# Moving the routing into the operand stage, single maximum items between the pieces of expert tiles, and half of the spline weights formed by TensorE

## The chip, the cores and the metric

The kernel runs on one core of one Trainium2 chip. The metric is the time of one execution on the device in microseconds. Inputs and outputs are in the device's memory; the core has the engines TensorE (PE), VectorE (DVE), ScalarE (ACT) and GpSimd (POOL), and SyncE (SP), whose queue issues most transfers.

## The reference

Four layers act on a sequence batch of 4 by 1024 tokens with 256 channels. Each layer normalises its input and adds an attention and a feed-forward result to it. What bears on the change:

```python
# layer 0: x + attention(xn) + experts(xn)
sh_mid = gelu(xt @ Wsh_up[e]); shared_out = sum_e sh_mid @ Wsh_down[e]     # 2 shared experts
probs = softmax(xt @ W_router)                                            # 16 routed experts
top_v, top_i = top_k(probs, 2)
routed_out = sum over the two chosen experts: (gelu(xt @ Wrt_up[e]) * top_v) @ Wrt_down[e]
# layer 1, feed-forward: gate_w, up_w (1024 x 256) and down_w (256 x 1024) are read off control points
w = 0.5 * (2*p1 + (p2 - p0)*f + (2*p0 - 5*p1 + 4*p2 - p3)*f**2 + (3*p1 - p0 - 3*p2 + p3)*f**3)
```

Layers 2 and 3 (a recurrent mix with ternary weights; an attention with low-rank experts) are not touched.

## The kernel before

Each layer first brings its weights in, and then loops over the four sequences of the batch. A layer's loop is a row of stages; a stage is a block in which every engine has its own list of instructions, tied by semaphores, with a barrier of all engines at its end. 1024 tokens are 8 tiles of 128.

**Layer 0's loop** has three stages.
1. `attention_operands` normalises the tokens, turns them (`m.xn_t`), projects each tile to queries, keys and values (L417, TensorE), adds the bias (L438, L439) and rotates queries and keys (L464 to L469, VectorE), splits them in halves of lower precision (L507, L509 ScalarE; L537, L538 GpSimd), turns these (L403) and stores them (L487). TensorE issues in tile `t` the projection of `t` and the turn of `t - 2`.
2. `experts` does three things at once. `Routing` makes the router's logits (L1189), softmax, the two best experts of each token and from their counts the slot of each token in a list that is sorted by expert and padded to 32 tiles of 128 slots (L1222 to L1272 on VectorE in five parts, L1199 to L1206 on TensorE). GpSimd scatters the tokens into their slots in memory (L1450), the SP queue fetches slots and the weights of each slot tile's expert (L1457, L1463). The shared experts run on all tokens (`up`, L1313, `gelu`, L1389, `down`, L1323, and the additions, L1424). Then the 32 slot tiles go through their expert in 16 pairs: `tile_turn` (L1335), `tile_up_products` (L1346), Gelu (L1407), `tile_down` (L1356), copy (L1415), and the store. Third, `MaximumPass` finds the row maxima of the attention's scores: TensorE forms the scores of a pair of maps over up to 512 keys (L606 the mask, L610 the product) and VectorE reduces them (L642). There are 96 such items and 4 "turn" items (L595, L637), which bring the maxima of a group of maps in place. Items use two pairs of PSUM banks in turn, so an item's matmuls wait for VectorE to be done with the item before the last.
3. `attention` takes the scores again, applies the exponential and adds up the values; `combine` adds the routed experts' results.

The order is written out by hand. `share_out` spreads the 100 items over named places in the lists of TensorE, VectorE and SP:

```python
ahead = [(("route", i), LEAD, (4, 6)) for i in range(Routing.PARTS)] + [(("scatter",), WAITING, (4, 6))]
rest = len(mp.items) - LEAD * Routing.PARTS - WAITING
mp.share_out(ahead + [(("tiles", i), rest / (pairs + 2), (4, 6)) for i in range(pairs + 2)], 2)
```

With `LEAD` 2 and `WAITING` 20, two items stand in each of five places among the routing parts and the shared experts, 20 in the place in which the scatter runs, and the other 70 in the loop over tile pairs: about four in a row between `tile_up_products(i - 1)` and `tile_down(i - 2)`.

**Layer 1's `spline_weights`** runs once, ahead of the loop. The weights are a sum of six basis tiles of 128x256, each times one scalar per row. 24 units (16 for gate and up, two on one basis tile, and 8 for down, one each) are made one after the other: VectorE scales the first (L1539) and adds five more (L1541), TensorE turns the result (L1553), ScalarE copies it twice (L1564, L1565), GpSimd subtracts (L1572). The SP queue brings the basis tiles into a ring of two.

## Time and profile before

| | |
|---|---|
| median of 3 runs | 4731.2 us (4724.24 to 4739.67) |
| the profiled execution | 4727.96 us |
| its span, first to last instruction | 4726.2 us |
| busy in the span: TensorE, VectorE, ScalarE, GpSimd | 3558.2, 2655.8, 1832.9, 669.3 us |
| mean granted clock of TensorE | 0.874 of full speed |

A row of the trace gives an instruction's line in the kernel, its engine and operation, out<-in by the program's names, and times in us from the span's start. PE is a matmul, PEld the load of its weights. `x4` counts instructions; a matmul in 32-bit floats is two records. `[1.79 <-PE ps L610]` is the idle time of that engine ahead of the row and what ended it.

### The profile page before, as it was taken

The numbers are of one execution on the slowest core, as the hardware profiler recorded it, in microseconds if no ns is written. First come the engines' busy times: TensorE is split into PE (matmuls) and PEld (weight loads), VectorE is DVE, ScalarE is ACT, GpSimd is POOL, SyncE is SP. The second block draws the span as 40 slices with busy tenths as digits, with TensorE's granted clock in tenths as the row PEclk, the third lists the DMA queues.
The fourth block names the chain that finished last, engine by engine and source line by source line (L and its number), as shares of the span: only waits on it lengthen the run. The fifth ranks groups of instructions, "written<-read, shape, count | busy, mean of one in ns | idle before, by whom it ended". The sixth has DMA issues, their size and how long they took to land. (4 is left out here: it accounts for less than half of the span.)

```text
span 4726.2 us, 61082 instructions
## 1 busy us (share of the span) xinstructions
PE 3558.2 (75%) x22176; PEld 2132.8 (45%) x22176; DVE 2655.8 (56%) x5412; ACT 1832.9 (39%) x2729; POOL 669.3 (14%) x814
## 2 busy tenths in 40 slices
PE   5676766767358787786865777866897797797797
PEld 3424344243123636344352645645572572572573
DVE  5656566566664543645436446454763764664664
ACT  3272542725254362634512323322306306306306
POOL 2011110121110000001000202202230230230230
PEclk8897988879679998898986988978899899899899
DMA  3403204033300000000020000001000000000000
GB/s 108 136 25 112 81 27 149 29 99 95 119 26 1 10 10 10 10 1 19 1 69 9 9 9 18 0 18 59 15 1 10 10 1 10 10 1 10 10 1 10
DMA packets 133505, 159.37 MB, mean 34 GB/s; under 512 B 16160, under 2 KB 109856, under 8 KB 133152
## 3 DMA queue, kind: packets, MB, share of 16 engines
q1 hardware_dynamic: 121712, 132.18, 8.7%
q0 software_dynamic: 6144, 16.79, 1.1%
q10 hardware_dynamic: 5328, 6.30, 0.4%
q8 instruction: 180, 2.95, 0.3%
q14 instruction: 141, 1.16, 0.1%
HBM read 108.57 MB, written 47.19 MB: 33 GB/s over the span
## 5 line engine op out<-in xcount | busy, mean ns | idle before, releaser
L642 DVE TENSOR_REDUCE arena<-ps 128x2 f32<-128x1024 f32 (+3 forms) x768 | 694.7, 951 | 175.3 <-PE ps L610 172.2
L831 ACT ACTIVATE arena<-ps 128x1024 f32<-128x1024 f32 (+3 forms) x768 | 570.9, 813 | 74.3 <-PE ps L744 68.6
L912 DVE TENSOR_TENSOR arena<-arena,tri 128x256 f32<-128x256 f32 x512 | 211.8, 424 | 300.6 <-ACT arena L831 293.9
L761 PE MATMUL ps<-arena 128*17 128x512 f32 (+3 forms) x3072 | 334.0, 507 | 6.7 <-DVE arena L912 4.0
L831 ACT ACTIVATE attention<-ps 128x1024 f32<-128x1024 f32 (+3 forms) x384 | 287.9, 809 | 131.0 <-PE ps L744 130.9
L744 PE MATMUL ps<-arena 64*128 64x512 f16 (+3 forms) x1536 | 252.0, 343 | 105.7 <-ACT arena L831 65.3
L2027 ACT ACTIVATE arena<-ps 128x256 f32<-128x256 f32 x192 | 63.9, 381 | 616.2 <-PE ps L1969 576.5
L610 PE MATMUL ps<-arena 64*128 64x512 f16 (+3 forms) x1536 | 239.0, 348 | 68.6 <-DVE arena L642 68.0
L761 PE MATMUL ps<-attention 128*33 128x512 f32 (+3 forms) x1536 | 289.1, 499 | 0.0
L744 PEld LDWEIGHTS ps<-arena 64*128 64x128 f16 x1536 | 69.9, 93 | 447.8 <-ACT arena L831 375.1
L417 PE MATMUL ps<-arena 128*128 128x512 f32 (+1 forms) x768 | 267.0, 497 | 0.0
L2099 POOL TENSOR_TENSOR arena<-arena 128x256 f32<-128x256 f32 x192 | 139.3, 725 | 511.2 <-DVE arena L2052 511.2
L1957 PE MATMUL ps<-arena 128*128 128x256 f32 x768 | 207.5, 393 | 1.8 <-DVE arena L2052 1.8
L1008 PE MATMUL ps<-ffn_parts,weight_parts 128*128 128x512 f32 x768 | 188.3, 407 | 14.9 <-DVE ffn_parts L1090 14.9
L1126 DVE TENSOR_TENSOR ffn<-ffn,ps 128x512 f32<-128x512 f32 x128 | 87.4, 683 | 195.3 <-ACT ffn L1071 117.7
L417 PEld LDWEIGHTS ps<-arena 128*128 128x128 f32 x768 | 143.5, 194 | 101.3 <-issue 94.9
L912 DVE TENSOR_TENSOR attention<-attention,tri 128x256 f32<-128x256 f32 x256 | 103.1, 424 | 144.0 <-ACT attention L831 143.8
L1008 PEld LDWEIGHTS ps<-ffn_parts,weight_parts 128*128 128x128 f32 x768 | 149.0, 195 | 54.0 <-DVE ffn_parts L1090 17.8
L606 PE MATMUL ps<-mask_col,mask_row 64*128 64x64 bf16 x2048 | 118.1, 198 | 67.5 <-DVE arena L642 66.8
L606 PEld LDWEIGHTS ps<-mask_col,mask_row 64*128 64x128 bf16 x2048 | 69.7, 96 | 191.2 <-DVE arena L642 129.0
L1957 PEld LDWEIGHTS ps<-arena 128*128 128x128 f32 x768 | 137.6, 189 | 37.3 <-issue 15.6
L1071 ACT ACTIVATE ffn<-ps 128x512 f32<-128x512 f32 x128 | 76.0, 594 | 198.0 <-PE ps L1008 198.0
(301 smaller groups left out, 6701.5 us busy)
## 6 DMA issues: line engine op xcount, KB each, us to landing
arena<-w_experts SPq DMA_DIRECT2D x128, 256.0 KB, 3.2
arena<-slots_x SPq DMA_DIRECT2D x32, 512.0 KB, 4.4
slots_y<-arena SPq DMA_DIRECT2D x32, 512.0 KB, 4.1
x_next<-sums SPq DMA_DIRECT2D x15, 1024.0 KB, 5.4
sums<-arena SPq DMA_DIRECT2D x24, 512.0 KB, 2.8
making<-basis SPq DMA_DIRECT2D x16, 768.0 KB, 4.5
x_next<-x SPq DMA_DIRECT2D x5, 1024.0 KB, 5.8
slots_x<-arena SPq DMA_DIRECT2D x1, 4096.0 KB, 15.3
```

The costliest lines, as they stand in the source:

```text
L417: last = pe.matmul(m.ps[:, 2 * (t % 2) + j, 0:w], m.xn_t[:, k, t * P:(t + 1) * P], wqkv[:, k, c0:c0 + w], start=(k == 0), stop=(k == KD - 1))
L606: pe.matmul(out[:, odd, w - P + H * i:w - P + H * i + H], m.mask_row[half, i, :], m.mask_col[half, i, half], start=(i == 0), stop=False, s ...
L610: last = pe.matmul(out[:, odd, 0:w], a.q[half, pair, qt * P:(qt + 1) * P], a.k[half, pair, c * CH:c * CH + w], start=not diag, stop=True, ...
L642: dve.reduce_max(a.mp[:, 2 * j:2 * j + 2, qt, c], out[:, :, 0:w], AX.X).then_inc(self.pair_out, 1)
L744: last = pe.matmul(m.ps[:, 4 + 2 * (v % 2) + odd, q0:CH], a.k[half, pair, kt * P:(kt + 1) * P], a.q[half, pair, c * CH + q0:(c + 1) * CH], ...
L761: last = pe.matmul(m.ps[width * hh:width * hh + w, unit % 2, q0:CH], a.v[:, kt, vh, :], a.p[:, (pairs * n + hh // 2) % ring, hh % 2, q0:CH ...
L831: act.activation(a.p[:, v % ring, :, q0:CH], m.ps[:, b:b + 2, q0:CH], ACT.Exp, scale=HD ** -0.5).then_inc(exped, 1)
L912: dve.tensor_tensor(diag, diag, keep, ALU.min).then_inc(masked, 1)
L1008: last = pe.matmul(m.ps[:, 2 * (n % 3) + j, :], w[wp][:, k, i * P:(i + 1) * P], f.x[:, xp, k, c * CH:(c + 1) * CH], start=(k, (wp, xp)) == ...
L1126: dve.tensor_tensor(f.inter[:, n % 3, :], f.gate[:, n % 2, :], m.ps[:, 2 * (n % 3) + 1, :], ALU.mult).then_inc(gated, 1)
L1957: pe.matmul(part(n, j), wt[:, k, i * P:(i + 1) * P], m.xn_t[:, k, columns(q)], start=(j == 0 and k == 0), stop=False, skip_group_check=True)
L2099: pool.tensor_tensor(f.h[:, r, n % 3, :], f.h[:, r, n % 3, :], f.wb[:, r, columns(q)], ALU.mult).then_inc(weighted, 1)
```

## The change

- The constants `LEAD` and `WAITING` go; `AHEAD` is 7.
- `Routing` runs in `attention_operands` when it is given: the logits on TensorE ahead of the projection of tile 2, in free columns of a bank of that projection; parts 0 to 3 on VectorE at the ends of tiles 2 to 5; the exponential on ScalarE behind tile 2; the rank matmuls behind the projection of tile 7; part 4 behind VectorE's last tile.
- `experts` begins with the scatters (GpSimd) and the weight and slot fetches (SP). The shared experts have four places of seven items, and each iteration over tile pairs has four places, between halves of `tile_up` and of `tile_down`, with one item in most of them.
- Buffers move: the routing's behind the operand stage's scratch, `f.mid` behind the attention's memory, the slots onto that scratch.
- In `spline_weights` every second unit is formed by TensorE: VectorE writes six diagonal matrices (the identity times a scalar per row) and TensorE multiplies the six basis tiles by them into one sum, which comes out turned. Four PSUM banks in place of two, a ring of four basis tiles in place of two.

```diff
@@ attention_operands
             norm.tensor(pe)
             pe.wait_ge(*weights)
             for t in range(NT):
...
                 if t == 2:
                     pe.wait_ge(norm.stored, NT // 2)
+                    if routing is not None:
+                        routing.tensor_logits(pe)
+                if t == 4 and routing is not None:
+                    pe.wait_ge(routing.shifted, 1)
...
+            if routing is not None:
+                pe.wait_ge(taken, 2 * (NT - 1))
+                routing.tensor_ranks(pe, 0)
             for t in range(NT - lag, NT):
                 turn(t)
...
+                if routing is not None and 2 <= t < 6:
+                    routing.vector(dve, t - 2)
+            if routing is not None:
+                routing.vector(dve, 4, 0)
...
+                if t == 2 and routing is not None:
+                    routing.scalar(act)
@@ experts
-        ahead = [(("route", i), LEAD, (4, 6)) for i in range(Routing.PARTS)] + [(("scatter",), WAITING, (4, 6))]
-        rest = len(mp.items) - LEAD * Routing.PARTS - WAITING
-        mp.share_out(ahead + [(("tiles", i), rest / (pairs + 2), (4, 6)) for i in range(pairs + 2)], 2)
+        ahead = 4 * AHEAD
+        rest = len(mp.items) - ahead
+        mp.share_out([(("shared", i), AHEAD, (4, 6)) for i in range(4)] +
+                     [(("tiles", i, p), rest / (4 * pairs + 4), (4, 6)) for i in range(pairs + 1) for p in range(4)], 1)
...
-            routing.tensor_logits(pe)
             pe.wait_ge(*weights)
             up(0, 0)
-            mp.tensor_share(pe, ("route", 0))
             up(0, 1)
-            mp.tensor_share(pe, ("route", 1))
+            mp.tensor_share(pe, ("shared", 0))
             up(1, 0)
             up(1, 1)
+            mp.tensor_share(pe, ("shared", 1))
             down(0)
-            mp.tensor_share(pe, ("route", 2))
+            mp.tensor_share(pe, ("shared", 2))
             down(1)
-            mp.tensor_share(pe, ("route", 3))
-            routing.tensor_ranks(pe, 0)
-            mp.tensor_share(pe, ("route", 4))
-            mp.tensor_share(pe, ("scatter",))
+            mp.tensor_share(pe, ("shared", 3))
             pe.wait_ge(added, NT)
             for i in range(pairs + 2):
                 if i < pairs:
                     tile_turn(i)
                 if 1 <= i <= pairs:
-                    tile_up_products(i - 1)
-                mp.tensor_share(pe, ("tiles", i))
+                    tile_up(i - 1, 0)
+                mp.tensor_share(pe, ("tiles", i, 0))
+                if 1 <= i <= pairs:
+                    tile_up(i - 1, 1)
+                mp.tensor_share(pe, ("tiles", i, 1))
                 if i >= 2:
-                    tile_down(i - 2)
+                    tile_down(i - 2, 0)
+                mp.tensor_share(pe, ("tiles", i, 2))
+                if i >= 2:
+                    tile_down(i - 2, 1)
+                mp.tensor_share(pe, ("tiles", i, 3))
...
             pool.wait_ge(m.slots_zeroed, 16)
-            pool.wait_ge(routing.placed, 1)
...
-            for part in range(Routing.PARTS):
-                mp.sync_share(sp, ("route", part))
-            sp.wait_ge(routing.tiles_known, 1)
             for i in range(4):
                 fetch_weights(i)
-            mp.sync_share(sp, ("scatter",))
             sp.wait_ge(m.scattered, 16 * 2 * NT)
             for g in range(4):
                 fetch_slots(g)
+            for i in range(4):
+                mp.sync_share(sp, ("shared", i))
@@ spline_weights, vector
             for i, (n, win, out) in enumerate(units):
-                dve.wait_ge(basis_in[n % 2], 16 * (n // 2 + 1))
-                if i >= 2:
-                    dve.wait_ge(turned, i - 1)
+                if i >= 4:
+                    dve.wait_ge(turned, i - 3)
+                if i % 2 == 1:
+                    for s in range(NSEG):
+                        ins = dve.tensor_scalar(f.diag[:, i // 2 % 2, s, :], m.ident[:, :], win[:, s:s + 1], None,
+                                                ALU.mult)
+                    ins.then_inc(spread, 1)
+                    continue
+                dve.wait_ge(basis_in[n % ring], 16 * (n // ring + 1))
...
@@ spline_weights, tensor
+                else:
+                    pe.wait_ge(basis_in[n % ring], 16 * (n // ring + 1))
+                    pe.wait_ge(spread, i // 2 + 1)
+                    for k in range(KD):
+                        for s in range(NSEG):
+                            last = pe.matmul(m.ps[:, i % 4, k * P:(k + 1) * P],
+                                             f.basis[:, n % ring, s, k * P:(k + 1) * P], f.diag[:, i // 2 % 2, s, :],
+                                             start=(s == 0), stop=(s == NSEG - 1))
                 last.then_inc(turned, 1)
```

## Rows read from the trace of the kernel before

**Rows 1.** Stretches: operand stage, experts stage of the first and second batch.
```profile
core 0: us, PE busy (x) PEld busy (x) DVE busy (x) ACT busy (x) POOL busy (x), PEclk, DMA share, GB/s
23.00:72.30 49.30, 33.72 (x208) 22.52 (x208) 36.00 (x74) 30.77 (x35) 14.78 (x20) 0.94 0.09 31
72.30:230.00 157.70, 106.72 (x832) 70.38 (x832) 101.89 (x167) 30.58 (x56) 15.71 (x16) 0.80 0.41 128
372.30:527.00 154.70, 104.00 (x832) 67.90 (x832) 101.89 (x167) 30.56 (x57) 15.42 (x16) 0.82 0.42 130
```

**Rows 2.** Order of time, front of the experts stage, first batch.
```profile
80.80 3.42 PE L1313 MATMUL ps<-arena 128*128 128x512 f32 x4
...
87.05 3.70 PE L1313 MATMUL ps<-arena 128*128 128x512 f32 x8
...
104.19 1.31 POOL L1450 DMA_INDIRECT slots_x<-arena  x1 [35.76 <-DVE arena L1267]
...
123.51 0.96 POOL L1450 DMA_INDIRECT slots_x<-arena  x1 [0.30 <-issue]
...
132.06 1.09 PE L1335 MATMUL ps<-ident,arena 128*128 128x128 f32 x4 [6.74 <-DMA arena<-slots_x]
```

**Rows 3.** Stretch of the logits, L1189 alone: TensorE, weight loads, granted clock.
```profile
73.95:80.95 7.00, 6.97 (x32) 6.90 (x32) 0.50 0.50 153
```

**Rows 4.** Groups from 132 to 222: count, busy, mean ns, idle before.
```profile
L642 DVE TENSOR_REDUCE arena<-ps 128x2 f32<-128x512 f32 (+3 forms) x67 | 60.4, 956 | 32.2 <-PE ps L610 31.9
```

**Rows 5.** Order of time in one iteration over tile pairs.
```profile
161.93 0.60 PE L1335 MATMUL ps<-ident,arena 128*128 128x128 f32 x4
...
162.37 1.06 PE L1346 MATMUL ps<-arena 128*128 128x128 f32 x8
...
163.36 0.39 PE L610 MATMUL ps<-arena 64*128 64x512 f16 x2
...
163.79 1.56 DVE L642 TENSOR_REDUCE arena<-ps 128x2 f32<-128x1024 f32 x2 [1.79 <-PE ps L610]
...
165.68 1.13 PE L1356 MATMUL ps<-arena 128*128 128x256 f32 x4
...
166.64 0.60 PE L1335 MATMUL ps<-ident,arena 128*128 128x128 f32 x4
```

**Rows 6.** Order of time in the first operand stage.
```profile
32.76 7.91 PE L417 MATMUL ps<-arena 128*128 128x512 f32 x24
...
45.56 1.07 PE L403 MATMUL ps<-ident_h,arena 128*128 128x128 f16 x16 [0.17 <-POOL arena L538]
...
45.82 0.69 DVE L469 TENSOR_TENSOR arena<-arena 128x512 f32<-128x512 f32 x1
...
65.18 0.69 DVE L469 TENSOR_TENSOR arena<-arena 128x512 f32<-128x512 f32 x1
```

**Rows 7.** Stretches of routing part 4 on VectorE, and all five parts' sum.
```profile
100.72:104.94 4.22, 0.39 (x6) 0.14 (x6) 3.88 (x15) 0.00 (x0) 0.75 (x1) 0.92 0.00 0
sum 8.59, PE 4.76 PEld 2.70 DVE 8.02 ACT 2.11 POOL 0.75; mean PE 0.95 PEld 0.54 DVE 1.60 ACT 0.42 POOL 0.15
```

**Rows 8.** The instructions of L467: duration ns, least, median and most.
```profile
L467 DVE TENSOR_TENSOR arena<-arena,sin x64: 416/884/889, 37.6 to 4414.8; 128x256 f32<-128x256 f32 x64
```

**Rows 9.** Stretch from VectorE's last record to the attention's first.
```profile
223.90:230.10 6.20, 0.77 (x2) 0.08 (x2) 0.01 (x1) 0.64 (x2) 0.00 (x0) 0.50 0.26 87
```

**Rows 10.** Groups of VectorE in the spline stage.
```profile
L1541 DVE SCALAR_TENSOR_TENSOR making<-making 128x256 f32<-128x256 f32 x120 | 65.9, 549 | 4.3
...
L1539 DVE TENSOR_SCALAR making<-making 128x256 f32<-128x256 f32 x24 | 8.4, 349 | 24.8 <-DMA making<-basis 24.8
```

**Rows 11.** Order of time: first and last record of the spline stage's work.
```profile
1229.56 0.35 DVE L1539 TENSOR_SCALAR making<-making 128x256 f32<-128x256 f32 x1 [18.42 <-DMA making<-basis]
...
1314.58 0.72 POOL L1572 TENSOR_TENSOR weight_parts<-making,weight_parts 128x256 fp32r<-128x256 f32 x1 [3.88 <-ACT making L1565]
```

**Rows 12.** Two stretches of 4 us, among items and in the loop: granted clock.
```profile
112.00:116.00 4.00, 1.69 (x18) 0.68 (x16) 3.62 (x5) 0.00 (x0) 2.96 (x4) 0.50 0.97 347
148.00:152.00 4.00, 2.90 (x28) 1.87 (x28) 3.18 (x4) 0.81 (x3) 0.00 (x0) 1.00 0.59 156
```

More of the change, by code:

```diff
@@ L1337, in tile_turn @@
                 last.then_inc(turned, 1)
-            def tile_up_products(i):
-                pe.wait_ge(weights_in[i % 4], 32 * (i // 4 + 1))
-                pe.wait_ge(turn_kept, i + 1)
-                if i >= 1:
-                    pe.wait_ge(tile_gelued, i)
-                for half in range(2):
-                    for k in range(KD):
-                        last = pe.matmul(m.ps[:, 1, half * P:(half + 1) * P], f.w_tile[:, i % 4, half, k * F0:(k + 1) * F0],
-                                         f.slots_t[:, i % 2, k, half * P:(half + 1) * P], start=(k == 0),
-                                         stop=(k == KD - 1))
-                last.then_inc(tile_upped, 1)
@@ new lines, in tile_down @@
+            def tile_down(i, half):
+                if half == 0:
+                    pe.wait_ge(tile_gelued, i + 1)
+                    if i >= 2:
+                        pe.wait_ge(kept, i - 1)
+                last = pe.matmul(m.ps[:, 2 + i % 2, half * D:(half + 1) * D], f.tile_mid[:, i % 2, half * P:(half + 1) * P],
+                                 f.w_tile[:, i % 4, half, KD * F0:EXPERT], start=True, stop=True)
+                if half == 1:
+                    last.then_inc(tile_downed, 1)
@@ L1426, in _ @@
             mp.vector_start(dve)
-            routing.vector(dve, 0)
-            mp.vector_share(dve, ("route", 0))
-            routing.vector(dve, 1)
-            mp.vector_share(dve, ("route", 1))
-            routing.vector(dve, 2)
+            mp.vector_share(dve, ("shared", 0))
+            mp.vector_share(dve, ("shared", 1))
             add(0)
-            mp.vector_share(dve, ("route", 2))
-            routing.vector(dve, 3)
+            mp.vector_share(dve, ("shared", 2))
             add(1)
-            mp.vector_share(dve, ("route", 3))
-            routing.vector(dve, 4, 0)
-            mp.vector_share(dve, ("route", 4))
-            mp.vector_share(dve, ("scatter",))
+            mp.vector_share(dve, ("shared", 3))
             for i in range(pairs + 2):
-                mp.vector_share(dve, ("tiles", i))
+                for part in range(4):
+                    mp.vector_share(dve, ("tiles", i, part))
         @block.gpsimd
@@ L1484, in _ @@
                     fetch_weights(i + 2)
-                mp.sync_share(sp, ("tiles", i))
+                for part in range(4):
+                    mp.sync_share(sp, ("tiles", i, part))
                 if i >= 3 and i % 2 == 1:
@@ L1523, in _ @@
             for n, (kind, t) in enumerate(tiles):
-                if n >= 2:
-                    last_use = max(i for i, u in enumerate(units) if u[0] == n - 2)
-                    sp.wait_ge(formed, last_use + 1)
+                if n >= ring:
+                    sp.wait_ge(turned, max(i for i, u in enumerate(units) if u[0] == n - ring) + 1)
                 src = basis_gu[t] if kind == "gu" else basis_d[t // 4][t % 4]
-                sp.dma_start(f.basis[:, n % 2, :, :], src).then_inc(basis_in[n % 2], 16)
+                sp.dma_start(f.basis[:, n % ring, :, :], src).then_inc(basis_in[n % ring], 16)
         @block.vector
@@ L2204, in program @@
             f.tile_weights = ar.take(SLOT_TILES, dtype=U32)
-            at = ar.at
-            f.mid = ar.take(E_SH * NC, CH)
-            ar = Arena(arena, at)
+            f.mid = Arena(arena, a.end).take(E_SH * NC, CH)
+            ar = Arena(arena, a.free)
             f.slots = ar.take(4, 4, D)
@@ L2236, in program @@
                 f.win = ar.take(3, F1 // P, NSEG)
-                f.basis = ar.take(2, NSEG, D)
+                f.basis = ar.take(4, NSEG, D)
+                f.diag = ar.take(2, NSEG, P)
                 f.w = ar.take(2, D)
```

97 lines of the change are left out of this document (51 added, 46 removed).

## The prediction

> **What bounds the kernel now.** I read the stretches by stage first, then the order of time inside the experts stage, then the groups of VectorE, then the granted clock in short stretches. The change touches the first layer, whose batch loop runs four times, and one stage of the second layer that runs once. One batch of the first layer takes an operand stage of 49.3 us, an experts stage of 157.7 us (154.7 us in the second batch) and an attention stage [rows 1]. The experts stage is over half of the batch, and in it no engine is full: VectorE works 101.9 us, TensorE 106.7 us, GpSimd 15.7 us [rows 1].
>
> The order of time says why. The stage opens with 7.0 us of router logits on TensorE, in which VectorE has nothing [rows 3]. The slots of the tokens are known only at 104.2, where GpSimd starts sixteen scatters that end at 124.5, and TensorE stands 6.7 us until the first slots are back at 132.1 [rows 2]. Up to there the pairs of expert tiles can't begin. From 132 on the stage is a loop over 16 pairs. In it VectorE has 67 maximum reductions of 0.956 us in the mean and is idle 32.2 us ahead of them, always for L610 [rows 4] (6.7 us of that is the slot wait again, so 25.5 us are the loop's own). One iteration shows where they come from [rows 5]: TensorE turns (0.44 us, start to start), makes the two up products (0.99), issues four items in a row, of which the third and fourth wait for VectorE to free a PSUM pair, and makes the down products (0.96). While the 2.4 us of tile work run, VectorE has two items left and then stands 1.8 us. The iteration takes 4.71 us. So the loop is bound by neither engine, but by their taking turns.
>
> **The operand stage.** VectorE sets its pace: from its L469 at 45.82 to the one five tiles on at 65.18 are 3.87 us a tile, without a gap; but TensorE too has only 0.17 us of slack per tile [rows 6]. After the last rotation at 65.18 come copies, transposes and stores to 72.3 [rows 1, 6]: 6.4 us in which VectorE is free.
> Added here are the logits, ahead of the third projection, and routing parts 0 to 3 on VectorE after tiles 2 to 5. These parts took 8.59 less 4.22, that is 4.37 us [rows 7]. The logits are 32 records, 6.97 us at half clock [rows 3], so an estimate of 3.5 us at the full one. TensorE ends its third projection at 40.67, and VectorE is ready for it when its L469 one tile before 45.82 ends, at 42.6 [rows 6]: 1.9 us are covered, 1.6 stay as a new wait of VectorE at tile 2. The exponential waits on ScalarE behind `high(2)`; with its table load it keeps ScalarE some 1.6 us from `store(1)`, which is wanted a tile later, and that tile has just been stretched by as much. It costs nothing, and at most 1.6 us. The rank matmuls (under 1 us) stand between two `turn`s in a gap of the tail. Part 4, 4.22 us, runs in the 6.4 us after the last rotation: free. Sum +6.0 us per batch; from +4.4 (logits hidden) to +10 (the clock falls in the logits and one or two projections run at half speed).
> L467 takes 0.42 us at the least and 0.88 us in the median, where GpSimd's subtraction runs beside it [rows 8]; part 4 now meets the last two such subtractions, and a VectorE instruction of 0.3 to 0.7 us could hold each back. I leave this inside the bound. The Trainium skill, SBUF — State Buffer, section "SBUF: two separate sides", says that the two engines share a port pair which one holds for a whole instruction; by it the tail would be 0.5 to 1.4 us longer, some 4 us over four batches, and the trace agrees on the doubled duration.
>
> **The experts stage.** I rebuild it from VectorE. Its 101.9 us lose the routing's 8.0 busy us [rows 1, 7]: 93.9. Added to that are its idle times:
> - At the start the first two up products. One took 3.42 us at half clock, two took 3.70 at the full one [rows 2]: 1.9 to 3.4 for the second, with the first item 6.4 us in all.
> - The shared part is now blocks: seven items, 3.7 us of TensorE work, seven items, and so on, three such blocks. While one runs VectorE finishes one or two items, and stands about 2.1 us: 6.3. Between blocks TensorE is lightly used; with some of the work at half clock another 3 (0 to 6).
> - The scatters start at once. They take 20.3 us as now (104.2 to 124.5), the landing and the fetch of the slots 7.6 as now (to 132.1): ready 28 us into the stage. The shared part has 28 items by 0.956, the additions and the idle above, 42 us. So the slot wait, 6.7 us now, goes, with 14 us to spare. The weight fetches and `x_next` are now in the queue in front; at the 312 GB/s that 128 GB/s at a share of 0.41 stands for [rows 1], those 3.1 MB take 10 us, also inside the margin.
> - In the loop an item stands between any two pieces. TensorE's work in an iteration is 0.44 + 0.99 + 0.96 and four items of about 0.25, 3.4 us; VectorE's is four items, 3.8 us. The longest piece ahead of an item is turn and half an up product, 0.93 us, about one reduction. What stays is a short hand-over around the narrow items, an estimate of 0.1 us for each of the 68: 7 (0 to the 25.5 of now). TensorE comes in at half clock and, at some 6 us per iteration there, is behind until it rises: 3 (0 to 6).
> - The end. From VectorE's last record to the next stage's first is 6.2 us [rows 9], with the last turn 7.
> Sum 93.9 + 6.4 + 6.3 + 3 + 7 + 3 + 7 = 126.6 us. Before it is 157.7 and 154.7 less the 1.7 us of barrier ahead of the first record, mean 154.5. Saved 27.9, less 6.0, that is 21.9 per batch and 88 in all.
>
> **The spline weights.** Now 24 units, each one L1539 and five L1541 on VectorE (0.349 and five by 0.549), from 1229.56 to 1315.3, 85.7 us [rows 10, 11]. L1539 waits 24.8 us for basis tiles, 18.4 of them for the first, so 6.4 us inside the stretch; the rest is a pace of 3.2 us a unit. After, every second unit is six 128x128 scalings on VectorE. A 128x256 one takes 0.349; a row of half the width isn't there, so 0 to 0.349 bounds each, and I take 0.24, 1.45 us a unit. A pair of units is 4.7 us on VectorE, twelve are 56. TensorE has per pair two transposes and twelve matmuls: 24 records of 0.22 us at half clock (6.97 by 32), 5.3 us and 0.7, and about half of that at the full one. It would be the slower at half clock, but is then full. The ring of four tiles takes the waits away but for some 2 us. With start and end (the last unit's matmuls, 3 to 5 us, are bare) 65 us against 85.7: 20 saved, from 6 (half clock throughout, 12 by 6 and the ends) to 28.
>
> **Sum.** The profiled execution took 4728.0 us, its span 4726.2; the median is 4731.2, 0.07% above. 4728 - 88 - 20 = 4620.
>
> **The rivals.**
> - *Better hand-over.* No idle in the loop and no slow clock: 126.6 - 7 - 3 - 3 = 113.6, operand stage +4.4: 36.5 by 4 and 28 are 174, so 4554. For it: one item per piece fits almost exactly. Against: narrow items can't hide 0.93 us of TensorE.
> - *Half clock in half of the loop.* An iteration is then about 6.4 us by TensorE in place of 4.1. Eight of them cost 18, less the 3 counted: 142 us, so 6.5 by 4 and 20 are 46: 4682. For it: the clock is 0.50 while TensorE is busy 1.7 of 4 us between items [rows 12]. Against: with 2.9 of 4 it is 1.00 there.
> - *The tiles' weights or slots come too late.* Shorter iterations fetch the same bytes. If landing takes the iteration back to 5 us, only the front of the stage gains: 140 us, 4674. Against: share 0.41 now [rows 1], and only the first slots are waited for.
> - *Slower: TensorE at half clock all through the loop.* The place is the loop, the price 2.3 us per iteration. 17 iterations and the shared blocks (8 us) give 126.6 + 36 + 8 = 171, so 16 + 6 lost per batch, 6 won in the splines: 4810. It decides from 12 of 17 iterations at half clock, since 12 by 2.3 by 4 are the 108 us won. In the logits TensorE is busy without a break and still at 0.50 [rows 3], so being busy is not enough. The Trainium skill, TensorE: Matmul & The Clock Gate, "HAM oscillation — how this bites in real kernels", has idle gaps bring the slow state back each time; gaps in the loop get shorter and more frequent, so it speaks rather for the fast state, and the row from 148 on agrees.
> - *No change*, by several of the bounds at once.
>
> **How the numbers follow.** Forecast 0.52 (its own range 4590 to 4650), better hand-over 0.16, half clock in part 0.13, late transfers 0.07, slower 0.05, no change 0.03, and between the cases 0.04. The range of 4560 to 4680 reaches to the good case and to the half-clock one. A measurement tells 0.3%, 14 us, from no change. Faster 0.92, same 0.03, slower 0.05.
>
> **What would show it.** Operand stage 55 us in place of 49, with a wait of VectorE for L417 at tile 2 and part 4 ahead of the stage's last copies. Scatters in the first 21 us of the experts stage, no wait of TensorE for slots. In the loop iterations near 4.2 us with VectorE over 90% busy and the clock at 1.00. In the spline stage a TensorE that is busy most of the time. The prediction is wrong if VectorE still stands over 1 us per iteration, if the clock is 0.50 beyond the first iterations, or if the operand stage grows over 10 us.

## The result, and the profile after

The changed kernel takes 4620.9 us in the median of 4 runs (4615.4 to 4623.7), against 4733.0 us (4 runs, 4724.2 to 4739.7) of the kernel before, measured beside it. The ratio is 0.9763, with a 95% interval of 0.9744 to 0.9782: 2.4% faster. The profiled execution took 4622.5 us, its span 4620.8 us.

In the kernel after, lines are L448 and L449 for the bias, L474 to L479 for the rotation, L1205 for the logits, L658 for the maximum, L626 for the scores of an item, L1326 and L1336 for the shared products, L1348, L1359 and L1369 for turn, up and down of the expert tiles, L1440 for the additions.

Stretches of the kernel after: operand stage and experts stage of the first batch [rows 1], then the second split at the first turn and at the end of the last long group of maximum items.

```profile
core 0: us, PE busy (x) PEld busy (x) DVE busy (x) ACT busy (x) POOL busy (x), PEclk, DMA share, GB/s
23.00:76.30 53.30, 38.10 (x256) 27.90 (x256) 42.18 (x120) 32.37 (x37) 14.20 (x20) 0.91 0.08 29
76.30:205.80 129.50, 103.65 (x784) 60.14 (x784) 94.84 (x121) 28.94 (x53) 15.74 (x16) 0.91 0.50 155
78.00:123.30 45.30, 32.11 (x185) 16.69 (x185) 26.59 (x39) 3.67 (x5) 15.74 (x16) 0.80 0.48 163
123.30:196.60 73.30, 69.43 (x589) 42.31 (x588) 65.56 (x78) 24.07 (x46) 0.00 (x0) 0.99 0.56 166
196.60:205.80 9.20, 2.11 (x14) 1.14 (x13) 2.69 (x6) 1.20 (x2) 0.00 (x0) 0.88 0.17 59
```

The same split of the kernel before:

```profile
80.80:132.10 51.30, 31.04 (x212) 15.03 (x213) 37.65 (x87) 5.26 (x7) 15.71 (x16) 0.70 0.30 100
132.10:220.40 88.30, 66.77 (x578) 47.29 (x578) 61.43 (x74) 23.44 (x47) 0.00 (x0) 0.91 0.49 152
220.40:230.10 9.70, 2.09 (x12) 1.24 (x13) 2.70 (x6) 0.64 (x2) 0.00 (x0) 0.67 0.17 56
```

VectorE's idle time is a row's length less its busy time. In the loop, the second row of the split, VectorE was idle 26.9 us and is idle 7.7. (The later batches differ less: the second batch's loop took 85.4 us before, and 73.4 after.) In the first row it was idle 13.7 and is idle 18.7, but it has 11 us less to do there, and the 7 us of logits ahead of the row are gone. The operand stage is 4.0 us longer. One iteration of the loop, in order of time, in place of [rows 5]:

```profile
158.51 0.66 PE L1348 MATMUL ps<-ident,arena 128*128 128x128 f32 x4
159.00 0.61 PE L1359 MATMUL ps<-arena 128*128 128x128 f32 x4
...
159.61 0.22 PE L626 MATMUL ps<-arena 64*128 64x128 f16 x2
159.76 0.71 PE L1359 MATMUL ps<-arena 128*128 128x128 f32 x4
...
160.68 0.70 PE L1369 MATMUL ps<-arena 128*128 128x256 f32 x2
160.79 0.69 DVE L658 TENSOR_REDUCE arena<-ps 128x2 f32<-128x512 f32 x1 [0.42 <-PE ps L626]
...
162.64 0.55 PE L1348 MATMUL ps<-ident,arena 128*128 128x128 f32 x3
```

It takes 4.13 us in place of 4.71, and VectorE's gaps are 0.4 us or less. The front of the experts stage, in place of [rows 2]:

```profile
78.04 6.73 PE L1326 MATMUL ps<-arena 128*128 128x512 f32 x8 [3.94 <-PEq L64]
...
78.97 1.31 POOL L1459 DMA_INDIRECT slots_x<-arena  x1 [6.81 <-issue]
...
98.32 0.96 POOL L1459 DMA_INDIRECT slots_x<-arena  x1 [0.30 <-issue]
99.09 6.07 PEld L1336 LDWEIGHTS ps<-arena 128*128 128x128 f32 x16 [0.25 <-issue]
99.09 6.47 PE L1336 MATMUL ps<-arena 128*128 128x256 f32 x16
101.58 2.04 SPq L1466 DMA_DIRECT2D arena<-slots_x  x4
102.91 0.76 DVE L1440 TENSOR_TENSOR arena<-ps,arena 128x256 f32<-128x256 f32 x2 [3.02 <-PE ps L1336]
```

The scatters run beside the shared experts, the slots are fetched at 101.6, and the loop starts at 123.3 without a wait for them.

Over four batches the saving reads off one mark in SP's queue, the issue of `x_next<-sums` that ends the fourth batch. Before it stands at 1215.15 and after at 1126.76: 88.4 us. From there to the issue of `making<-lq`, which follows the spline stage, are 101.1 us before (to 1316.29) and 83.6 after (to 1210.37): 17.5 us. The spans of the two traces differ by 105.4 us, their medians by 112.

### The profile page after: what moved, and what is told of

It is laid out like the page before. It is cut to its first block and busy times, and to the rows that moved or that the text cites. A ratio compares the mean times of both kernels' runs of the same rounds, so it can differ in the third digit from the quotient of the medians.

```text
span 4620.8 us, 61585 instructions
## 1 busy us (share of the span) xinstructions
PE 3602.9 (78%) x22440; PEld 2160.3 (47%) x22440; DVE 2635.4 (57%) x5412; ACT 1832.0 (40%) x2725; POOL 666.1 (14%) x814
## 5 line engine op out<-in xcount | busy, mean ns | idle before, releaser
L658 DVE TENSOR_REDUCE arena<-ps 128x2 f32<-128x1024 f32 (+3 forms) x768 | 696.7, 951 | 107.3 <-PE ps L626 102.8
L626 PE MATMUL ps<-arena 64*128 64x512 f16 (+3 forms) x1536 | 233.1, 329 | 31.0 <-DVE arena L658 30.1
L1983 PEld LDWEIGHTS ps<-arena 128*128 128x128 f32 x768 | 137.7, 189 | 37.2 <-issue 15.7
L2078 DVE TENSOR_TENSOR arena<-arena,ps 128x256 f32<-128x256 f32 x192 | 79.7, 415 | 123.0 <-ACT arena L2053 123.0
```

The lines of the kernel that those rows point to most:

```text
L626: last = pe.matmul(out[:, odd, 0:w], a.q[half, pair, qt * P:(qt + 1) * P], a.k[half, pair, c * CH:c * CH + w], start=not diag, stop=True, ...
L658: dve.reduce_max(a.mp[:, 2 * j:2 * j + 2, qt, c], out[:, :, 0:w], AX.X).then_inc(self.pair_out, 1)
L1983: pe.matmul(part(n, j), wt[:, k, i * P:(i + 1) * P], m.xn_t[:, k, columns(q)], start=(j == 0 and k == 0), stop=False, skip_group_check=True)
```

## The experiments

All times in this table are in us. "Mark" is the issue of `x_next<-sums`. "Loop" is the first batch's stretch from the first turn to the last long maximum group, with VectorE's idle time in it. Each kernel was timed beside the kernel before, whose median moved by up to 3 us from one time to the next; so differences of 3 us between medians in this table say nothing.

| kernel | median (runs) | mark | loop, idle |
|---|---|---|---|
| before | 4729.9 to 4733.2 (four times, 4 to 9 runs each) | 1215.2 | 88.3, 26.9 |
| after | 4620.9 (4) | 1126.8 | 73.3, 7.7 |
| spline_alone | 4708.3 (5) | 1213.6 | 84.2, 22.7 |
| items_alone | 4685.8 (4) | 1166.8 | 72.5, 9.5 |
| four_in_a_row | 4677.2 (4) | 1187.1 | 87.5, 22.7 |
| two_and_two | 4623.8 (4) | 1126.5 | 72.9, 7.5 |
| long_and_short | 4638.1 (4) | 1140.6 | 77.4, 12.4 |
| three_and_one | 4650.5 (4) | 1154.8 | 79.5, 14.0 |
| parts_late | 4639.9 (4) | 1145.8 | 73.4, 7.8 |
| fine_shared | 4590.7 (5) | 1094.7 | 74.9, 8.7 |
| diag_scalar | 4602.0 (5) | 1131.8 | 73.3, 7.9 |
| both | 4567.6 (5) | 1092.7 | 74.9, 8.5 |

### The three parts of the change, one at a time

**spline_alone** is the kernel before with the new `spline_weights` and its buffers. Of the edit only the buffers are shown:

```diff
...
-                f.basis = ar.take(2, NSEG, D)
+                f.basis = ar.take(4, NSEG, D)
+                f.diag = ar.take(2, NSEG, P)
```

> The kernel before with the new spline weights alone (diagonals and TensorE for half of the tiles, four basis buffers); routing and items stay as before. From the traces of before and after, the time from the first spline unit on VectorE to the last copy fell from 85.7 to 68 us. Theory (the three parts of the change add up): 17 us faster than before, 4716 us, within 4 either way. Rival (the spline's gain was partly that of another clock or of another arrival of the basis after the new fourth batch): under 10 us, 4723 or more.

Measured 4708.3, 4 us below the range of 4712 to 4720. The ratio is 0.9946 (0.9933 to 0.9960), that is 19 to 32 us by the runs. The profile gives the part itself: from mark to `making<-lq` 83.6 us, the same as in the changed kernel, so 17.5 us; the two traces' spans differ by 18.5. The theory holds for the stage; the medians moved by more than the traces account for, and that excess stays open.

**items_alone** is the kernel before with `tile_up` and `tile_down` in halves and an item place behind each. Routing and splines stay. Of the edit only the sharing out is shown:

```diff
...
-        mp.share_out(ahead + [(("tiles", i), rest / (pairs + 2), (4, 6)) for i in range(pairs + 2)], 2)
+        mp.share_out(ahead + [(("tiles", i, p), rest / (4 * pairs + 4), (4, 6)) for i in range(pairs + 1) for p in range(4)], 1)
```

> The kernel before with the interleaved item places in the loop of expert tiles alone; routing stays in the experts stage, spline weights stay as before. Theory: VectorE's idle time in the loop goes from 27.7 to about 8 us, 20 us per batch, 80 in all: 4650 to 4660 us; moving the routing is then worth the rest of what the experts and operand stages gained (88), about 2 us per batch net. Rival (the routing's move paid more than that, as VectorE's front part of the experts stage lost its routing operations of some 20 us while the operand stage took only 4): 4665 us or more.

Measured 0.9897 (0.9882 to 0.9913), 47 us; the mark moved by 48.4, 12.1 per batch. So the rival's time held. The theory's 20 us per batch were too many: the 27.7 us that I had read as the loop's idle time before reached to 223.9 and so had some 3 us behind the last items in it, the loop of this kernel still idles 9.5 us, and VectorE works 1.6 us more in it. The loop is 15.8 us shorter in the first batch, and 12.6 in the second (72.8 in place of 85.4). The slots are still waited for here, 6.7 us ahead of the loop. Its row:

```profile
132.50:205.00 72.50, 69.94 (x577) 42.47 (x578) 63.05 (x75) 24.04 (x46) 0.00 (x0) 0.96 0.61 185
```

**four_in_a_row** is the changed kernel with the four places put together:

```diff
                 if 1 <= i <= pairs:
                     tile_up(i - 1, 0)
-                mp.tensor_share(pe, ("tiles", i, 0))
-                if 1 <= i <= pairs:
                     tile_up(i - 1, 1)
-                mp.tensor_share(pe, ("tiles", i, 1))
+                for p in range(4):
+                    mp.tensor_share(pe, ("tiles", i, p))
                 if i >= 2:
                     tile_down(i - 2, 0)
-                mp.tensor_share(pe, ("tiles", i, 2))
-                if i >= 2:
                     tile_down(i - 2, 1)
-                mp.tensor_share(pe, ("tiles", i, 3))
```

> The changed kernel with the four item places of a pair of expert tiles put together again, between the up and the down products, as in the kernel before; routing in the operand stage and the new spline stay, and the number of items per pair stays. Theory (VectorE's idle time in the loop is hand-over: TensorE's products of 1.9 and 0.6 us lie in one piece while VectorE has nothing ready): VectorE's idle time in the loop goes from 7.8 back to about 26 us, so 17 to 20 us per batch, 70 to 80 in all: 4690 to 4700 us. Rival (the gain of the loop came from routing being gone and from TensorE's clock staying at 1.0, not from the order): under 5 us per batch, 4640 or less.

```profile
128.30:215.80 87.50, 65.86 (x586) 46.74 (x584) 64.85 (x79) 22.95 (x46) 0.00 (x0) 0.93 0.45 139
```

Measured 4677.2, 56 us above the changed kernel: 14 per batch, between the theory's 17 to 20 and the rival's 5, and nearer the theory. The idle time came back, 22.7 us in the first batch and 20.9 in the second. 4.4 us of the 56 are a lower clock in the operand stage of the first batch (last section). The order of the items is thus worth some 52 us by the medians on top of the routing's move, and 56 by the marks (60.3 less 4.4); without the move it is worth 48. By the marks, routing in the operand stage alone gave 28.1, or 32.5 without those 4.4; items alone gave 48.4; together they gave 88.4. The 7.5 us more than the sum are 1.9 per batch, and nothing here says from what. The granted clock of this loop is 0.93, against 0.99 in the changed kernel; what part of the 14 us is the clock's was not separated.

### How many items, and where

**two_and_two** moves the places to behind the up products and behind the down products, two items each. Against four_in_a_row:

```diff
                     tile_up(i - 1, 1)
-                for p in range(4):
-                    mp.tensor_share(pe, ("tiles", i, p))
+                mp.tensor_share(pe, ("tiles", i, 0))
+                mp.tensor_share(pe, ("tiles", i, 1))
                 if i >= 2:
                     tile_down(i - 2, 0)
                     tile_down(i - 2, 1)
+                mp.tensor_share(pe, ("tiles", i, 2))
+                mp.tensor_share(pe, ("tiles", i, 3))
```

> The changed kernel with the items of a pair of tiles in two places of two: two between the up and the down products, two after the down products. Two theories of what counts. A (only the longest unbroken stretch of TensorE's other products against the 1.9 us that VectorE has in hand with two bank pairs counts): turns and ups together are about 1.9 us of 4.2, downs about 0.5, so one long stretch per pair of tiles outlasts what VectorE has in hand by about 1 us; with 18 pairs about 10 to 14 us idle per loop rather than 7.8: 4630 to 4645 us. B (idle grows with the number of items in a row, four giving 26 and one 8): two give about 14 to 17, 4645 to 4660 us. C (order matters little): 4625 or less.

Measured 4623.8: C. Theory A fell by an error of its own: turn and up products are 1.43 us [rows 5], not 1.9. With the right figure it gives what was measured, since 1.43 and an item's 0.25 are within the 1.9 us of two reductions; but that figure was put in after the result. The next two kernels ask whether that sum predicts.

**long_and_short**: the two halves are unequal, 1.9 us of products in one stretch and 0.5 in the other, two items behind each.

```diff
                 if 1 <= i <= pairs:
                     tile_up(i - 1, 0)
                 mp.tensor_share(pe, ("tiles", i, 0))
+                mp.tensor_share(pe, ("tiles", i, 1))
                 if 1 <= i <= pairs:
                     tile_up(i - 1, 1)
-                mp.tensor_share(pe, ("tiles", i, 1))
+                mp.tensor_share(pe, ("tiles", i, 2))
+                mp.tensor_share(pe, ("tiles", i, 3))
                 if i >= 2:
                     tile_down(i - 2, 0)
-                mp.tensor_share(pe, ("tiles", i, 2))
-                if i >= 2:
                     tile_down(i - 2, 1)
-                mp.tensor_share(pe, ("tiles", i, 3))
```

> The changed kernel with the items again two and two, but the places moved: downs, turn and the first up product (1.9 us) in one stretch, two items, the second up product (0.5 us), two items. Theory (the stretch with the first item behind it, against two items in hand of 1.9 us): 0.25 us short per pair of tiles, some 4 us per batch, 4637 us (4630 to 4645). By the same sum four in a row are 2.4 + 0.25 - 1.9 = 0.75 us short, 13 us over 17 pairs of tiles, and its loop measured 13.5 us longer. Rival (two items in a row are as good as one wherever they stand): 4624 or less.

Measured 4638.1, loop 77.4: 4.1 us longer than the changed kernel's, as the sum said.

**three_and_one**: three items behind the up products, one behind the down products. Against two_and_two:

```diff
                 mp.tensor_share(pe, ("tiles", i, 1))
+                mp.tensor_share(pe, ("tiles", i, 2))
                 if i >= 2:
                     tile_down(i - 2, 0)
                     tile_down(i - 2, 1)
-                mp.tensor_share(pe, ("tiles", i, 2))
                 mp.tensor_share(pe, ("tiles", i, 3))
```

> The changed kernel with three items after the up products and one after the down products. The runs so far: with one item between any two pieces, and with two and two, VectorE is idle 7.5 to 7.7 us in the loop; with four in a row 20.9 to 22.7. Theory (what counts is that TensorE's stretch, with the first item behind it, is no longer than what VectorE still has in hand, two items of 0.95 us in the mean): turn and ups take 1.43 us start to start and downs 0.96. The longest run with little between is downs, one item, turn and ups, then an item: 0.96 + 0.25 + 1.43 + 0.25 = 2.9 us, against the two items in hand and the one made between, 2.85. So hardly any new idle time, 0 to 2 us per batch: 4621 to 4630 us. Rival (each gap of VectorE comes with how many items stand in a row, and three are nearer to four than to two): 8 to 10 us per batch, 4655 to 4665.

Measured 4650.5, loop 79.5: 6.2 us longer. The theory fell, and the rival is nearer but not right either (it asked for 8 to 10 us, and for 4655 or more). The order of time shows the step that it left out:

```profile
159.20 4.38 DVE L658 TENSOR_REDUCE arena<-ps 128x2 f32<-128x1024 f32 x4 [1.11 <-PE ps L626]
160.48 0.39 PE L626 MATMUL ps<-arena 64*128 64x512 f16 x2 [1.10 <-DVE arena L658]
160.80 1.13 PE L1369 MATMUL ps<-arena 128*128 128x256 f32 x4
```

The third item of a row finds no free PSUM pair, so TensorE stands 1.10 us in front of it, with the down products queued behind. Then it makes the item (0.39 us), in which VectorE already works on what it has. So VectorE has in hand two reductions less the making of the last, 1.5 us rather than 1.9, and less again where a narrow one is among them (they range from 0.40 to 1.23 us). This step is read from the order of time, and no kernel tests it: put into the sum for two and two (1.43 and 0.25 against 1.5), it asks for some 3 us more per batch, and that loop is not longer. TensorE's whole wait for VectorE in the loop tells the five orders apart:

| order | TensorE waits for VectorE | loop |
|---|---|---|
| one by one | 3.7 us | 73.3 |
| two and two | 8.2 | 72.9 |
| long and short | 11.6 | 77.4 |
| three and one | 16.5 | 79.5 |
| four in a row | 21.1 | 87.5 |

Its work in an iteration is 3.4 us against 3.8 of VectorE, some 7 us of slack in 17 iterations. By this account waits up to about that are free, and what lies beyond comes back: 11.6, 16.5 and 21.1 less 7 are 5, 9 and 14 us, where the loop grew by 4, 6 and 14. The account was made from these five traces, after the runs; it foretold none of them, and is 3 us off for three and one. The kernel before fits it as well, with 21.0 us of such waits and a loop of 88.3 us.

### The operand stage

**parts_late** leaves routing part 0 after tile 2 and puts parts 1 to 3 behind the last tile (and on TensorE, not shown, the rank products behind the last turn).

```diff
-                if routing is not None and 2 <= t < 6:
-                    routing.vector(dve, t - 2)
+                if routing is not None and t == 2:
+                    routing.vector(dve, 0)
             if routing is not None:
+                for part in range(1, 4):
+                    routing.vector(dve, part)
                 routing.vector(dve, 4, 0)
```

> The changed kernel with only the first routing part left after tile 2 of the operand stage; parts 1 to 3 come after the last tile on VectorE, and the rank products after all turns of TensorE. In the changed kernel the last rotation starts 3.7 us later than before, though 1.6 us of waiting and 4.4 us of routing were put ahead of it; the two products with the sine take 9.1 us in the stage rather than 12.5. Theory (they run beside GpSimd's subtraction of the tile before and are held by it; a routing part between them lets GpSimd finish first, so four parts cost VectorE less than their own time): with the parts gone from the tiles the two groups return to 11.5 to 12.5 us, and the last rotation starts near 67 (68.86 in the changed kernel, 65.18 before), not at 65.5, where it would be if 3.7 us were what the parts cost. Parts 1 to 4, about 8 us, then stand behind it and the stage ends 0.5 to 2 us later: 4623 to 4629 us. Rival (the routing parts simply took less time there than in the experts stage): the two groups stay near 9.1 us.

Rows of one tile in the changed kernel, after a routing part, and then its last tile, which no part precedes:

```profile
59.85 0.42 DVE L475 TENSOR_TENSOR arena<-arena,sin 128x256 f32<-128x256 f32 x1
60.19 0.42 DVE L477 TENSOR_TENSOR arena<-arena,sin 128x256 f32<-128x256 f32 x1
...
66.94 0.80 POOL L553 TENSOR_TENSOR arena<-arena 128x256 f16<-128x256 f32 x1 [2.60 <-ACT arena L523]
67.25 0.77 DVE L475 TENSOR_TENSOR arena<-arena,sin 128x256 f32<-128x256 f32 x1
67.70 0.84 POOL L554 TENSOR_TENSOR arena<-arena 128x256 f16<-128x256 f32 x1
67.94 0.88 DVE L477 TENSOR_TENSOR arena<-arena,sin 128x256 f32<-128x256 f32 x1
```

The two products with the sine over the first stage, changed kernel and then parts_late (least, median and most in ns):

```profile
L475 DVE TENSOR_TENSOR arena<-arena,sin x8: 425/599/777, 37.5 to 67.2; 128x256 f32<-128x256 f32 x8
L477 DVE TENSOR_TENSOR arena<-arena,sin x8: 411/418/885, 37.9 to 67.9; 128x256 f32<-128x256 f32 x8
```

```profile
L475 DVE TENSOR_TENSOR arena<-arena,sin x8: 424/774/778, 38.4 to 69.4; 128x256 f32<-128x256 f32 x8
L477 DVE TENSOR_TENSOR arena<-arena,sin x8: 410/883/886, 38.7 to 70.1; 128x256 f32<-128x256 f32 x8
```

The medians are back at 0.77 and 0.88 with the parts gone, and the two groups take 11.2 us in place of 9.1, just short of the 11.5 to 12.5 that the theory asked for. In the third batch (operand stage from 597 on), where the projections run alike in both kernels, the first to the last rotation are 30.6 us apart in the changed kernel and 28.5 in parts_late: parts 1 to 3, which take 3.9 us, cost 2.1. So the theory holds on where the time went. The last rotation can't be compared in the first batch, where the clock fell (last section). The Trainium skill, SBUF — State Buffer, section "SBUF: two separate sides", has VectorE and GpSimd exclude each other on a shared port pair for a whole instruction. These rows agree in direction, 0.42 us apart from the subtraction and 0.77 and 0.88 beside it; that the wait is a whole instruction they do not show.

The kernel is 19 us slower, where I had forecast 2 to 8. Split by stage, the move itself fits: where no clock falls, attention and operand stage together take 149.4 us (211.2 to 360.6) against 148.5 (205.8 to 354.3), 0.9 more. The rest goes with TensorE's granted clock, in places that the edit did not touch: 4.4 us each ahead of the third projection's end in the first and the fourth batch, and some 6 us together in the experts stages of the second and the third. First, second and third batch's loop of parts_late:

```profile
128.60:202.00 73.40, 69.53 (x590) 42.34 (x588) 65.65 (x79) 24.04 (x46) 0.00 (x0) 0.99 0.54 166
407.00:483.80 76.80, 73.54 (x590) 44.84 (x588) 65.88 (x79) 24.04 (x46) 0.00 (x0) 0.91 0.50 159
688.50:763.90 75.40, 71.92 (x590) 43.74 (x588) 65.69 (x79) 24.04 (x46) 0.00 (x0) 0.94 0.53 162
```

The changed kernel has 73.3 or 73.4 in all four batches. Whether the edit had a part in the clock's falls is open; without this split the 19 us would have been booked as the price of the move.

### The shared part, the diagonals, and both

**fine_shared**: twelve pieces and twelve places. Each pair of additions also comes as soon as its products are there, and TensorE's wait for them moves behind the up products of the loop's third iteration. Of the edit only the down products are shown:

```diff
...
-            down(0)
-            mp.tensor_share(pe, ("shared", 2))
-            down(1)
-            mp.tensor_share(pe, ("shared", 3))
-            pe.wait_ge(added, NT)
+            for n in range(NT):
+                down(n // TC, n % TC)
+                mp.tensor_share(pe, ("shared", 4 + n))
```

> The changed kernel with the shared experts' products cut into twelve pieces (four up products, eight token tiles of the down product) and the same 28 items spread over twelve places between them, in place of seven after each of four blocks; each addition comes as soon as its two down products are there, and TensorE waits for the additions only ahead of the loop's first tile down product. From the first up product to the first turn the changed kernel takes 45.3 us, in which VectorE works 26.6. Theory (the 18.7 us idle is the start, 5 to 7 us, and the blocks of 3.7 to 6.7 us that outlast what VectorE has in hand): 36 to 40 us, 6 to 9 per batch, 4590 us (4582 to 4600). Rival 1 (TensorE at half clock sets this part, its granted clock is 0.80 there, and shorter pieces keep it at 0.50): 44 us or more, 4615 or above. Rival 2 (the slots are then waited for: the loop comes 5 to 9 us sooner, the scatters end 24 us before the loop now): no gain over 4610, and a wait of TensorE for the slots shows.

```profile
82.40:116.10 33.70, 28.10 (x185) 12.72 (x185) 25.63 (x38) 3.59 (x5) 15.71 (x16) 0.89 0.64 219
116.10:191.00 74.90, 70.27 (x589) 42.81 (x588) 66.25 (x79) 24.07 (x46) 0.00 (x0) 0.98 0.53 163
```

Measured 4590.7 (ratio to before 0.9703, 0.9690 to 0.9716), the forecast time, though the part was to take 36 to 40 us. It takes 33.7 us in place of 45.3, 11.6 less; the loop gives 1.6 back, and some of the rest goes to the operand stage of the first batch, where the clock fell (last section). 10.6 us of the 11.6 are VectorE's idle time, 18.7 to 8.1. Most of that is the additions: VectorE's waits for the down products went from 8.2 us to 0.6, its waits for items from 10.2 to 7.3. How much came from the shorter pieces and how much from the earlier additions was not tested apart. The granted clock of the part rose from 0.80 to 0.89, and the down products show where: in blocks the first was sixteen records of 6.47 us, here it is four records of 1.13 us in seven pieces of eight (2.07 in the other). Nothing waits for slots. Rival 1 is refuted: the clock went up and not down.

**diag_scalar**: the scalings for the diagonals on ScalarE.

```diff
...
-                        ins = dve.tensor_scalar(f.diag[:, i // 2 % 2, s, :], m.ident[:, :], win[:, s:s + 1], None,
-                                                ALU.mult)
...
+                    last = act.activation(f.diag[:, i // 2 % 2, s, :], m.ident[:, :], ACT.Copy,
+                                          scale=units[i][1][:, s:s + 1])
```

> The changed kernel with the 72 scalings of the spline weights' diagonals made by ScalarE, two units ahead of their use, so that VectorE only forms the even units. The spline stage takes 67 us from its first unit on VectorE to the last copy in the changed kernel: of it VectorE has 12 units of six diagonals (1.3 to 2.2 us each) and 12 of 3.1 us. Theory (VectorE sets the pace of the stage): a pair of units goes from about 5 to 3.5 us, 52 to 56 us, 12 to 15 gained: 4606 to 4610 us. Rival 1 (TensorE sets it: 24 records a unit of 2.9 us at full and 4.8 at half clock, two transposes and the first matmul's hand-over): 62 us or more, gain under 6. Rival 2 (ScalarE, which also makes the copies, is held by six more operations a unit and delays them): no gain or a loss.

```profile
1160.00:1180.00 20.00, 17.09 (x149) 16.44 (x148) 18.44 (x32) 17.30 (x60) 9.64 (x12) 1.00 0.74 234
```

Measured 4602.0 (0.9726, 0.9712 to 0.9739), 19 us less, where 11 to 15 had been forecast; from mark to `making<-lq` 69.3 us in place of 83.6, that is 14.3, as the theory said. (In the other traces with the change's spline stage this stretch takes 80.4 to 83.6 us, so the gain is known to some 3 us.) The mark itself comes 5.0 us later, since the clock fell in the first batch, and the remaining 6 us of the 15.5 between the spans lie behind the stage, where nothing was edited. VectorE set the pace of the changed kernel's spline stage: it was busy 19.3 us of the 20 from 1160 on. Now TensorE, VectorE and ScalarE are all over 85% busy in this row.

**both** holds these two edits together:

> The twelve pieces of the shared experts and ScalarE's diagonals together. Theory (they lie in different stages and add up): the sum of the two gains, 27 and 13 us, 4580 us. Rival (the earlier end of the fourth batch lets the first basis tiles be waited for longer in the spline stage): 5 to 10 us above the sum.

Measured 4567.6 us (4562.4 to 4572.3), ratio to before 0.9654 (0.9641 to 0.9668): 53 us below the changed kernel, against 30 and 19 for the parts. They add up within 5 us, and the rival, 5 to 10 us above the sum, did not come. That the time is 12 us below the 4580 of the forecast is in part the clock: it did not fall in this kernel's first operand stage, as it did in both parts'. This version beats both kernels.

## Why the prediction was right, point by point

Forecast 4620, measured 4620.9. So close a match is partly luck. The forecast took 108 us off a profiled execution of 4728.0; the traces differ by 105.4 us and the medians by 112. And terms were off in both directions:

| term | forecast | shown by | measured |
|---|---|---|---|
| operand stage, first batch | +6.0 | stretches | +4.0 |
| shared part, VectorE idle | 15.7 | stretch to the first turn | 18.7 |
| loop, VectorE idle | 10 | stretch of the loop | 7.7 |
| end | 7 | last stretch | 6.5 |
| experts stage, VectorE's work | 93.9 | three stretches | 94.8 |
| experts stage | 126.6 | sum | 127.8 |
| four batches | -88 | mark | -88.4 |
| splines | -20 | mark to `making<-lq` | -17.5 |

- **The loop bound by taking turns** was the right reading, and four_in_a_row and items_alone show it: the order alone is worth 48 to 56 of the 105 us. VectorE is 89% busy in the loop (65.56 of 73.30 us), a little under the 90% that was to show it; iterations take 4.1 to 4.3 us. What the prediction's picture lacked: single items aren't needed. Two and two does the same.
- **The clock in the loop** was 0.99. The three rivals that had TensorE at half clock or transfers late in the loop did not come; the DMA share was 0.56.
- **The logits** took 3.64 us at full clock against an estimate of 3.5, and VectorE's wait at tile 2 is 1.64 us against 1.6 (second row).

```profile
38.16 3.64 PE L1205 MATMUL ps<-arena 128*128 128x16 f32 x32
44.51 0.69 DVE L448 TENSOR_TENSOR arena<-ps,arena 128x512 f32<-128x512 f32 x1 [1.64 <-PE ps L424]
```

- **The operand stage** was mis-sized in its routing term: 4.37 us of parts at their full price, where VectorE gets back what it no longer loses to GpSimd in the tiles behind them. The prediction had this contention only in the tail, as a cost. There it did show (the two products L1278 took 1.44 us in place of 0.49 in parts_late), and cost nothing.
- **The shared part** was mis-sized by 3 us. The first item came after 6.9 us, not 6.4, and the blocks of down products took 6.47 and 5.36 us, where 3.7 had been counted for every block; the first of them ran in part at half clock. VectorE waited 8.2 us for them ahead of its additions.
- **The slots' wait** went, with 17 us to spare in place of 14: slots fetched from 101.6 on, some 4 us each, loop at 123.3. The 42 us of the prediction's sum are the 28 items and the idle time alone (26.8 and 15.7); the additions, 3.0 us in the trace, belong on top. That makes 45.5 us, against 45.3 measured.
- **The splines**: a scaling of 128x128 was taken at 0.24 us; the least is 0.27, and the mean 0.35, since it is held up to 0.79 us while GpSimd subtracts. Twelve units take 20.4 us in place of 17.4, 3 us more, which is about the 2.5 that were missing. VectorE also waits 3.3 us for basis tiles inside the stretch, where 2 had been counted.

```profile
L1550 DVE TENSOR_SCALAR making<-ident,making x72: 271/281/786, 1143.8 to 1202.3; 128x128 f32<-128x128 f32 x72
```

```profile
L1550 DVE TENSOR_SCALAR making<-ident,making 128x128 f32<-128x128 f32 x72 | 20.4, 353 | 0.0
```

## What to carry to other kernels

Where two engines hand work to each other through two buffers, compare the first engine's longest stretch of other work with what the second has in hand when that stretch starts: at most two pieces, and less by the making of the last where the first had to wait for a buffer. Then add up what the first waits in front of a full pair of buffers. In the five orders here, waits up to its slack were free and most of what lay beyond returned as idle time of the second. Large blocks of side work are worth cutting even where the totals balance, as the shared part's 11.6 us showed, together with taking up their results as soon as they are there. Small operations placed where another engine holds up yours may cost half of their own time.

## What was not expected of the hardware

- The same stretch of the operand stage ran at two clocks. The third projection of the first batch, behind the logits, took 2.8 us in the changed kernel and four of the others (granted clock 1.00), and 5.4 to 5.5 us in parts_late, four_in_a_row, fine_shared and diag_scalar, though the instructions ahead of it are the same. The clock fell to 0.50 already in the last 1.3 to 1.8 us of the logits, which took 4.2 to 4.5 us in this second group and 3.64 in the first. The two projections that open the stage tell the groups apart as well: they took 5.3 to 6.0 us in the first group and 6.3 to 6.6 in the second. In parts_late, the order of time and then its granted clock (PEclk) in single microseconds:

```profile
32.80 6.38 PE L424 MATMUL ps<-arena 128*128 128x512 f32 x16
39.02 4.35 PE L1207 MATMUL ps<-arena 128*128 128x16 f32 x32
43.21 5.47 PE L424 MATMUL ps<-arena 128*128 128x512 f32 x8
...
core 0: us, PE busy (x), PEclk, DMA share, GB/s
40.00:41.00 1.00, 1.00 (x11) 1.00 0.00 0
41.00:42.00 1.00, 1.00 (x10) 0.87 0.00 0
42.00:43.00 1.00, 1.00 (x7) 0.50 0.00 0
...
47.00:48.00 1.00, 1.00 (x3) 0.50 0.00 0
48.00:49.00 1.00, 1.00 (x11) 0.71 0.08 16
```

  VectorE waits 10.2 us for projections in such a stage, in place of 5.8: 1.0 us more ahead of the first and 3.4 ahead of the third. TensorE had been busy without a break from 32.8 on, so this fall had no gap before it. Why it comes is open, and differences of 5 us between two kernels here can be this alone. The prediction had it as the upper bound of the operand stage.
- With the shared products in shorter pieces, items between them and the additions earlier, the granted clock of that part was 0.89 in place of 0.80.
- Routing operations of 3.9 us on VectorE cost 2.1, since the products behind them no longer ran beside GpSimd's subtraction.
